# Quantised attention: ROUND added in the scaling step, one of four parts scaled on ScalarE, reciprocal issued before the next maximum

## The reference, cut to what matters

```python
def _fq(x, delta, zp, n_bits):
    xi = _round_ste(x / delta) + zp
    xq = jnp.clip(xi, 0.0, 2.0 ** n_bits - 1.0)
    return (xq - zp) * delta

def _attn(x, ctx, wq, wk, wv, wo, bo, dq, dk, dv, dw):      # H = 16 heads of 32
    ...
    sim = jnp.einsum('bhid,bhjd->bhij', _fq(q, dq, 128.0, 8), _fq(k, dk, 128.0, 8)) * SCALE
    attn = jax.nn.softmax(sim, axis=-1)
    out = jnp.einsum('bhij,bhjd->bhid', _fq(attn, dw, 0.0, 8), _fq(v, dv, 128.0, 8))
```

## Time and profile before

| what | us |
|---|---|
| median of three runs | 3182.81 (3182.1 to 3185.9) |
| the profiled execution, its own time | 3184.13 |
| its span, first to last instruction | 3182.3 |
| first part (two quantised attentions) | about 0 to 1365 of the span |
| a whole round in the loop, q1 fill to q1 fill | about 76.9 |
| mean granted TensorE clock | 0.955 |

### The profile page before, as it was taken

The page is one execution under the profiler, slowest core; times in us unless marked ns, Lnnn a source line. Parts: engine busy times, 40 slices in busy tenths (PEclk is TensorE's granted clock), DMA queues, the critical chain, the costliest instruction groups (busy, mean ns, idle before and its releaser), DMA issues. The chain is left out here.

```text
span 3182.3 us, 54635 instructions
## 1 busy us (share of the span) xinstructions
PE 2850.5 (90%) x18304; PEld 2290.7 (72%) x18304; DVE 1912.6 (60%) x4469; ACT 1453.1 (46%) x3747; POOL 773.1 (24%) x1179
## 2 busy tenths in 40 slices
PE   3688888888888887579999997999999999999997
PEld 2455555665565654359999997888888888888886
DVE  5599999999999999543333333534343433443432
ACT  3466666666666666321111111444444444444442
POOL 1222223322233232123333332211111111111110
PEclk8799999999999998779999998999999999999997
DMA  5233333333333333241000012101000000000000
GB/s 149 40 69 74 76 73 75 73 75 81 74 76 73 76 76 70 47 139 37 30 26 26 26 40 80 60 27 39 27 26 33 26 33 26 26 26 26 33 14 14
DMA packets 328217, 168.59 MB, mean 53 GB/s; under 512 B 276960, under 2 KB 293344, under 8 KB 328160
## 3 DMA queue, kind: packets, MB, share of 16 engines
q1 hardware_dynamic: 328160, 167.87, 21.0%
HBM read 75.54 MB, written 25.17 MB: 32 GB/s over the span
## 5 line engine op out<-in xcount | busy, mean ns | idle before, releaser
L585 ACT ACTIVATE e<-S,bias,qk_scale 128x256 f32<-128x256 f32 x1024 | 564.1, 563 | 141.7 <-DVE pq L692 137.8
L684 DVE TENSOR_SCALAR e<-e,rsum 128x256 f32<-128x256 f32 x1024 | 337.1, 391 | 2.9
L670 DVE TENSOR_REDUCE negmax<-S 128x4 f32<-128x1024 f32 x256 | 311.3, 1217 | 31.3 <-PE S L494 30.6
L1544 POOL TENSOR_TENSOR mid_partsB<-mid_actB,mid_partsB 128x256 fp32r<-128x256 f32 x128 | 101.6, 794 | 637.6 <-DVE mid_partsB L1449 637.6
L555 ACT ACTIVATE shifted<-PJ,round_col,inv 128x512 f32<-128x512 f32 x192 | 149.3, 778 | 215.8 <-PE PJ L162 197.1
L153 PE MATMUL PJ<-w_a_wo,oT 128*128 128x512 f32 x512 | 244.3, 622 | 2.6 <-ACT oT L594 1.8
L761 POOL TENSOR_TENSOR bias<-negmax,qk_scale 128x4 f32<-128x4 f32 x256 | 72.9, 285 | 628.9 <-DVE negmax L670 628.7
L162 PE MATMUL PJ<-hT,w_a_wq 128*128 128x256 f32 x1536 | 203.9, 290 | 24.1 <-DVE w_a_wq L415 19.7
L162 PEld LDWEIGHTS PJ<-hT,w_a_wq 128*128 128x128 f32 x1536 | 191.6, 195 | 37.2 <-issue 37.2
L162 PE MATMUL AG0A<-h_partsA,upA 128*128 128x256 f32 x1536 | 200.2, 287 | 7.3 <-POOL h_partsA L1539 3.4
L585 ACT ACTIVATION_READ_ACCUMULATOR e<-S,bias,qk_scale 128x1 f32 x1024 | 206.3, 201 | 0.0
(11 more groups left out here) (182 smaller groups left out, 5730.7 us busy)
## 6 DMA issues: line engine op xcount, KB each, us to landing
x_in<-in_x_dram SPq DMA_DIRECT2D x16, 512.0 KB, 3.8
ctx_in<-in_ctx_dram SPq DMA_DIRECT2D x16, 512.0 KB, 3.8
mid_dram<-x SPq DMA_DIRECT2D x16, 512.0 KB, 2.7
y_inA<-mid_dram SPq DMA_DIRECT2D x16, 512.0 KB, 3.5
part_dram<-x3A SPq DMA_DIRECT2D x16, 512.0 KB, 3.7
y_inB<-mid_dram SPq DMA_DIRECT2D x16, 512.0 KB, 3.5
kv_in<-in_ctx_dram SPq DMA_DIRECT2D x16, 512.0 KB, 4.4
baseB<-part_dram SPq DMA_DIRECT2D x16, 512.0 KB, 3.3
```

The costliest lines, as they stand in the source:

```text
L585: nc.scalar.activation(e[:, s, i, :], S[s][:, i // 2, i % 2, :], ACT.Exp, bias=bias[:, s, i:i + 1], scale=qk_scale[:, ph.a:ph.a + 1], accu ...
L670: nc.vector.tensor_reduce(negmax[:, g % 2, :], S[g % 2][:].rearrange("p i q n -> p (i q) n"), AX_X, ALU.max, negate=True).then_inc(max_don ...
L684: nc.vector.tensor_scalar(e[:, s, i, :], e[:, s, i, :], rsum[:, s, i:i + 1], WMAX, ALU.mult, ALU.min).then_inc(prob_scaled, 1)
L1544: nc.gpsimd.tensor_tensor(mid_parts[:, f % 2, 1, :], mid_act[:, f % 2, :], mid_parts[:, f % 2, 0, :], ALU.subtract).then_inc(mid_low_done, 1)
```

## The change

Four things, all in the first part:
- The final step of a probability was (e + ROUND) - ROUND after a scaling min(e * r, 255). Now the scaling is e * r + ROUND, and the last instruction is min(e - ROUND, 255).
- Of the four scalings of a group DVE does three (`DVE_SCALES = 3`); ACT does the fourth, as an Identity activation with scale and bias from columns (`act_scale`). It stands first in ACT's step g, for group g-1, ahead of shifts, `act_oT`, transposed fills and the exponentials of group g. It waits for the reciprocal. `pq` waits for it.
- The reciprocal of group g-1 is taken out of `dve_probs` and stands ahead of the maximum of group g+1 in DVE's step.
- Nothing else moves: POOL's, PE's and SP's lists are as before.

```diff
+            def act_scale(act, ph, g):
+
+                n = ph.group(g)
+                s = g % 2
+                act.wait_ge(rsum_done, n + 1)
+                for i in range(DVE_SCALES, 4):
+                    nc.scalar.activation(e[:, s, i, :], e[:, s, i, :], ACT.Identity, bias=round_col[:, 0:1],
+                                         scale=rsum[:, s, i:i + 1]).then_inc(prob_scaled_act, 1)
...
@@ act_phase, the same place in act_drain
+                    if g:
+                        act_scale(act, ph, g - 1)
+                    elif prev:
+                        act_scale(act, prev, GROUPS - 1)
                     for where in late(ph, prev, g):
                         if kind_of(where[2]) in QUANTISED:
                             act_shift(act, where)
...
+            def dve_recip(dve, ph, g):
+
+                n = ph.group(g)
+                dve.wait_ge(dsum_done, n + 1)
+                nc.vector.reciprocal(rsum[:, g % 2, :], dsum[:, g % 2, :]).then_inc(rsum_done, 1)
+
             def dve_probs(dve, ph, g, fills=()):
 
                 n = ph.group(g)
                 s = g % 2
-                dve.wait_ge(dsum_done, n + 1)
-                nc.vector.reciprocal(rsum[:, s, :], dsum[:, s, :]).then_inc(rsum_done, 1)
                 for where in fills:
                     dve_clip(dve, where)
                 dve.wait_ge(rsum_done, n + 1)
 
-                for i in range(4):
-                    nc.vector.tensor_scalar(e[:, s, i, :], e[:, s, i, :], rsum[:, s, i:i + 1], WMAX, ALU.mult,
-                                            ALU.min).then_inc(prob_scaled, 1)
+                for i in range(DVE_SCALES):
+                    nc.vector.tensor_scalar(e[:, s, i, :], e[:, s, i, :], rsum[:, s, i:i + 1], ROUND, ALU.mult,
+                                            ALU.add).then_inc(prob_scaled, 1)
                 for where in fills:
                     dve_unshift(dve, where)
-                dve.wait_ge(prob_scaled, 4 * (n + 1))
+                dve.wait_ge(prob_scaled, DVE_SCALES * (n + 1))
+                dve.wait_ge(prob_scaled_act, (4 - DVE_SCALES) * (n + 1))
                 if not (isinstance(n, int) and n < 2):
 
                     dve.wait_ge(probs_turned[s], turned_count(ph, g, 2))
-                nc.vector.tensor_scalar(pq[:, s], e[:, s], ROUND, ROUND, ALU.add,
-                                        ALU.subtract).then_inc(prob_quantised, 1)
+                nc.vector.tensor_scalar(pq[:, s], e[:, s], ROUND, WMAX, ALU.subtract,
+                                        ALU.min).then_inc(prob_quantised, 1)
...
@@ dve_phase
+                    if g:
+                        dve_recip(dve, ph, g - 1)
+                    elif prev:
+                        dve_recip(dve, prev, GROUPS - 1)
                     if g + 1 < GROUPS:
                         dve_max(dve, ph, g + 1)
```

More of the change, by code:

```diff
@@ L206, in build @@
         CTX_AT, HT_AT = 4, 7
+        DVE_SCALES = 3
         STATS_X_AT, XHAT_X_AT = 3, 5
@@ L396, in build @@
             prob_scaled = sem("prob_scaled")
+            prob_scaled_act = sem("prob_scaled_act")
             prob_quantised = sem("prob_quantised")
@@ L624, in act_drain @@
             def act_drain(act, ph):
+                act_scale(act, ph, GROUPS - 1)
                 for where in late(None, ph, 0):
@@ L752, in dve_drain @@
             def dve_drain(dve, ph):
+                dve_recip(dve, ph, GROUPS - 1)
                 dve_probs(dve, ph, GROUPS - 1)
@@ L969, in _ @@
                     ln_stats(dve, ln, x_in, 1)
+                    dve_recip(dve, P_A, GROUPS - 1)
                     dve_probs(dve, P_A, GROUPS - 1)
```

## The result

The changed kernel takes 3308.47 us (3304.76 to 3309.31, four runs) against 3182.86: a ratio of 1.0386, 95% interval 1.0373 to 1.0399. The forecast was 3258 with a range of 3202 to 3295: the sign was right, the loss is 125.6 us where 75 stood. Of it 123.7 lie in the first part: the first matmul of the second part starts at 1504.93 instead of 1381.25, and from there to the end it is 1802.6 us against 1801.1. A round in the loop settles at 85.33 instead of 76.9, so fourteen of them make 119. One of the four runs of the last experiment took 4549.44 us at a granted clock of 0.6, where the others have 0.96: it is the only slow run here, and nothing is read from it.

What follows compares the result with a forecast made beforehand. DVE, 93% busy in the loop, and PE were taken to set the pace in different steps; terms summed to +5.0 us a round (ends 3.5 and 6.5), +70 over fourteen, +75 in all: 3258 us, range 3202 to 3295.

Steps and rivals of the forecast that it cites:

- The mechanism: Everything behind ACT's scaling waits for DVE's reciprocal, closing a chain of 4.00 us a group with a shift, 3.32 without.
- the gains: Five DVE-bound steps behind place 2 each save a scaling of 0.28, plus two gaps of 0.12: -1.6 us a round.
- the clock: PE's idle at place 2 grows from 1.2 to 3.6, bringing one more clock fall: +1.3 us a round.
- ACT's scaling: The fourth scaling, put on ACT, was priced at 0.46 us, ends 0.35 and 0.6.
- Place 2: Phase 2, step 3: PE starts 2.4 late behind reciprocal, scaling, shift and `act_oT`, making DVE late: +2.3 us a round.
- Phase 2, step 7: PE is 2.8 late there but already idles 3.59: +0.3 us a round.
- Place 3: Phase 1, step 7: the fill hT waits for the later shift and DVE's turned step waits for it: +1.2 us a round.
- Phase 1, step 3: Wait for `act_oT` without POOL additions ahead; PE 0.9 late, half hidden behind DVE's statistics: +0.4 us a round.
- The light steps: Four PE-bound steps with a q or k fill take 3.73 where the chain needs 4.00: +1.1 us a round.
- rival A: Faster: busy time decides, the wait hides in ACT's waits for PE; 42 us off, 3141; chance 0.12.
- D: Worse: DVE's clip waits 0.3 for the later shift in 12 shift steps, +3.6 us a round more, 3305; chance 0.06.

Runs made afterwards that it cites:

- the last experiment: The changed kernel with 14, 14, 7 and 4 unread identity matmuls in four of PE's idles a round: 3263.54 us, ratio 1.0247.
- before, filled: The kernel before the change with 14 unread identity matmuls in PE's one long idle of a round: 3173.90 us, ratio 0.9962.
- changed, filled: The changed kernel with 14, 14, 8 and 5 unread identity matmuls in four of PE's idles a round: 3263.27 us, ratio 1.0248.

## Why the prediction was wrong in size

The start of PE's scores gives each step's length. One round in the loop of each kernel (us). Before the change a round takes 76.5 to 77.0, with 9.8 to 10.7 in phase 1, step 0; the one shown is a short one. The filled ones are rounds without a slow fill:

| step | before | changed | before, filled | changed, filled | difference of the filled |
|---|---|---|---|---|---|
| phase 2: 0 | 3.86 | 3.72 | 3.88 | 4.87 | +0.99 |
| 1 | 4.27 | 3.77 | 4.26 | 3.98 | -0.28 |
| 2 | 3.72 | 3.98 | 3.72 | 3.97 | +0.25 |
| 3 | 4.99 | 8.76 | 5.00 | 7.31 | +2.31 |
| 4, 5, 6 | 13.67 | 13.45 | 13.67 | 13.45 | -0.22 |
| 7 | 4.87 | 9.59 | 4.87 | 7.13 | +2.26 |
| phase 1: 0 | 10.27 | 5.30 | 8.96 | 6.37 | -2.59 |
| 1 | 3.72 | 5.25 | 4.06 | 5.49 | +1.43 |
| 2 | 3.72 | 3.97 | 4.19 | 3.98 | -0.21 |
| 3 | 5.00 | 7.16 | 4.99 | 5.76 | +0.77 |
| 4, 5, 6 | 12.17 | 12.17 | 12.17 | 12.17 | 0 |
| 7 | 6.24 | 8.21 | 6.26 | 6.92 | +0.66 |
| sum | 76.5 | 85.3 | 76.0 | 81.4 | +5.4 |

The mechanism held. What failed are three terms of the sum: phase 1, step 1, which it didn't have (1.4 us a round), the gains, which it put at 1.6 and which are 0.2, and the clock, for which it had one more slow fill a round and there are three more. Point by point:

- *What bounds the kernel, and the mechanism*: right but for one reading. Steps 4 and 5 of phase 2 take 5.57 and 4.28 before the change, after it and in the runs with less work on DVE, and PE has no idle in them (421.85 to 431.70 in the round of the earlier trace rows): there DVE did not set the pace alone. The wait shows as forecast (280 us of "over 200"), PE's idle ahead of `pe_pv` is 3.5 twice and 2.0 once a round, ACT's wait for PE fell from 159.9 to 72.7 but did not vanish, DVE waits for `dsum` and for scores. DVE's share fell to 81%, where I had 85.
- *ACT's scaling* 0.46, ends 0.35 and 0.6: 0.50 from start to start (446.79 to 447.29), 0.60 in all. The sentence on the Trainium skill, ScalarE: Activation LUTs, What ACT_TABLE_LOAD costs, had an estimate of 0.49; the trace agrees with it more closely than with the row that I took.
- *Place 2* (phase 2, step 3), +2.3: +2.31 without the clock. *Phase 2, step 7*, +0.3 for it and the long idle: 2.26 - 2.59 = -0.3. *Place 3* (phase 1, step 7), +1.2: +0.66. *Phase 1, step 3*, +0.4: +0.77. *The light steps*, +1.1: 0.99 - 0.28 + 0.25 - 0.21 = +0.75; the steps of 3.97 and 3.98 are the chain with a shift, which stood at 4.00. Together +4.2 against 5.3, before clock and gains (the filled kernels have tenths of their own in them).
- *Phase 1, step 1*: +1.43, not in the sum at all. DVE's list of step 0 is its longest (maximum, transposed fill, clip of v, scalings, `pq`), and the reciprocal of group 0, which ACT now needs before anything of step 1, stands behind it:

```profile
477.27 1.23 DVE L686 TENSOR_REDUCE negmax<-S 128x4 f32<-128x1024 f32 x1 [2.20 <-PE S L496]
...
483.67 0.17 DVE L693 RECIPROCAL rsum<-dsum 128x4 f32<-128x4 f32 x1
...
483.87 0.60 ACT L597 ACTIVATE e<-e,round_col,rsum 128x256 f32<-128x256 f32 x1 [2.08 <-DVE rsum L693]
```

  The exponentials of group 1 follow, and the scores of group 3 wait for them, 1.45 us (487.38). I had called the lateness of place 2's twin in step 7 covered by PE's long idle. On PE it was; through DVE's list it reached ACT. How much of the 1.43 is that lateness and how much the list itself no run separates: in the filled kernel, where that maximum doesn't wait, the scores still wait 1.71. That is a miss of 1.4 a round, 20 us.
- *Gains*, -1.6 in the five steps behind place 2: -0.2 in steps 4 to 6. There DVE stands idle before the maximum (2.71 at 454.01), and PE's own 5.56, 4.29 and 3.6 set the pace. I had subtracted savings on DVE in steps from which my own place 2 had taken the bound away. The runs without the wait have them, 28 to 31 us, the rival A's 42 in a smaller size, but not step by step: about half arrive at PE's long idle, where phase 1, step 0 takes 9.3 instead of 9.8 to 10.7. That idle is gone in the changed kernel. Missed: 1.4 a round, 20 us.
- *PE's clock*, +1.3 for one fall more. Four fills a round are slow instead of one stretch of about 1.3. In 4.50, 5.40, 4.40 and 4.50 us of the four slow stretches the granted clock is:

```profile
449.00:453.50 4.50, 4.50 (x26) 4.42 (x24) 1.31 (x5) 2.42 (x9) 0.20 (x1) 0.62 0.38 72
471.40:476.80 5.40, 5.40 (x14) 3.81 (x12) 3.68 (x9) 2.20 (x7) 1.60 (x3) 0.50 0.25 49
494.10:498.50 4.40, 4.40 (x26) 4.29 (x24) 2.59 (x9) 2.35 (x9) 1.09 (x3) 0.64 0.31 60
428.80:433.30 4.50, 4.47 (x12) 3.35 (x12) 4.24 (x9) 2.66 (x10) 2.13 (x2) 0.62 0.00 0
```

0.50 is the lower level (1.2 GHz) throughout; the others are a mixture with the upper. I had let the clock fall only after an idle as long as the one seen before, 3.59. It also fell after 1.97 (and 1.45 two steps before), and after 1.35 and 0.76 with little between them. The kernel before has idles of 1.20 alone, and of 0.72 and 0.76 close together, with no slow fill behind them; no idle of its loop lies between 1.20 and 3.57. Behind the loop one does, which I had not looked at: at 1251.69 scores take 0.61 instead of 0.39 us behind an idle of 2.49, and from 1248 to 1264 the granted clock averages 0.61. I should have put both ends for each of the four places: none or four falls, 0 to 5 us a round. The length of the idle doesn't decide by itself either. In one of the first rounds of the changed kernel the same 3.46 us stand before a fill at the full clock:

```profile
386.38 0.40 PE L517 MATMUL O<-pT,vQ 128*32 128x256 bf16 x4 [3.46 <-ACT oT L605]
386.71 3.06 PE L162 MATMUL PJ<-w_a_wv,hT 128*128 128x512 f32 x12
```

and in the pair of rows above, a fill behind 1.76 is at full speed and one behind 1.63 is slow. By the filled kernels the clock's part of the difference is 45 - 12 = 33 us, about 39 with the slow fills that are left in six rounds of the changed kernel with filler (1.15 each) and one of the kernel before with it (0.9), and 18 stood in the sum: missed 15 to 21 us.

In totals, between the filled kernels 3263.3 - 3173.9 = 89 us are order and waits, 83 without their slow fills, where 57 stood (70 + 5 less 18 for the clock): 20 and 20 missed, 16 put too high. With the clock's 33 that makes 122 of 125.6; the rest is that the kernel before measured 3182.86 in one series and 3185.92 in the other. The two misses in the chain alone would have made about 3283, that of the clock alone 3273 to 3279, both inside the range; together they left it. Its far end, 6.5 us a round, allowed two falls where four places could have one. D, the rival on that side, was a wrong one (the clip's wait: 25 us of rows in all, inside the chain) with 6%; by its own terms (3258 and 14 x 3.6) it stood at 3308, not at 3305, and that this is the measured number is chance. Rival A was refuted as written, busy shares don't decide; but its sign is what comes when shift and `act_oT` don't stand behind the wait (3162) or there is no wait (3156), with 22 and 28 us of its 42. Here the Trainium skill, Perfetto Trace Analysis, Optimizing Scalar/DVE Operations, that a saturated DVE may justify moving work to Scalar, holds in one order of ACT's list (3162.5), fails in another (3308.5) and is void in a third (3185.5).

Open: the part of the clock that is hidden or comes back as waits is only known by the filled kernels; what besides an idle's length makes the next fill slow; and whether it is more than chance that two kernels of different work have a round of 85.33. The order with the reciprocal left behind the maximum and ACT's scaling first was not tried: there DVE's transposed fill would wait for a bank that ACT empties only behind the reciprocal, which stands behind that fill on DVE.

## What to carry to other kernels

Before work is moved to an engine with time to spare, ask what is queued behind it there and when its input comes: in an engine that works in order, a half-microsecond instruction with a late input, put first, costs what stands behind it. Put it as late as its reader allows: here the same instructions took 3308, 3162 or 3185 us by their place alone. When a change makes TensorE idle in more places, price each place with the clock's fall too, and don't subtract savings on an engine in steps where the loss has just taken the bound away from it.

## What the runs showed of the hardware that was not expected

- A matmul of the identity, fp32, 128x128 by 128 columns, takes 0.23 us (24 in 5.6, as 48 rows), a transpose of the same size 0.13 (8 in 1.02 to 1.09).
- In the settled rounds of the changed kernel the fills behind idles of 3.5 us, of 2.0, and of 1.35 and 0.76 close together run at a granted clock of 0.50 to 0.64 (0.50 is 1.2 GHz) and take 1.2 to 2.5 us longer; after single idles of 1.20 no fill in the kernel before is slow. But one fill behind 3.46 (386.71) and those behind 1.76 in another kernel take their full-clock 3.06 and 3.14.
- An ACT instruction of one column that only waits for the reciprocal costs as much (3307) as the whole change (3308), with nothing taken off DVE. The scaling's work of 0.50 us is hidden where it doesn't wait (3156, against 3154 with none of it); behind the wait it is not (3308, against 3257 with one column of it).
